# A two-layer graph attention kernel: paired differences on GpSimd in layer 1, and mended orders in four other places

## The reference

```python
# layer 0, 8 heads of 64
data1 = (h @ W.T + b).reshape(N, H, D)
e = src.T[:, :, None] + trg.T[:, None, :]          # per head, N x N
e = where(e >= 0, e, 0.01 * e) + adj[None]          # adj is added, values up to 1e9
x = x + softmax(e) @ data1
# layer 1, 8 heads of 64
adj = maximum(adj, eye(n))
atts = q @ k.T / 8 - 1e16 * (1 - adj)
x = x + sum over heads of softmax(atts) @ values @ Wo
```

## Time and profile before

| | us |
|---|---|
| Median of 3 runs | 4567.05 (4562.28 to 4569.85) |
| The profiled execution, device time | 4565.15 |
| Its span, first to last instruction | 4563.2 |
| Busy PE, DVE, ACT, POOL | 4340.7, 3659.2, 3251.4, 3423.3 |
| Granted TensorE clock, mean | 0.983 |

### The profile page before, as it was taken

How to read it: one execution, slowest core, us unless ns; L and a number is a source line. 1 busy time by engine, 2 the same in 40 slices (tenths; PEclk the granted TensorE clock), 3 DMA queues, 4 the chain that set the end, 5 groups by cost and what they waited for, 6 DMA issues and landing times.

```text
span 4563.2 us, 111741 instructions
## 1 busy us (share of the span) xinstructions
PE 4340.7 (95%) x42956; PEld 2097.1 (46%) x42956; DVE 3659.2 (80%) x7790; ACT 3251.4 (71%) x6022; POOL 3423.3 (75%) x2955
## 2 busy tenths in 40 slices
PE   8699999999999978969999999999999999999998
PEld 4222222222222223425666656656656566566565
DVE  5498998989989854438888888878888878888886
ACT  5366666666666642318888878888878888888886
POOL 2466776677766740009999989989989999899897
PEclk9899999999999989989999999999999999999999
DMA  3566667667666535452333433433433334334333
GB/s 143 138 214 199 201 215 212 215 202 218 222 193 206 158 123 154 118 153 78 114 115 93 127 96 99 135 102 101 120 106 114 111 91 127 107 98 130 100 110 104
DMA packets 464215, 646.06 MB, mean 142 GB/s; under 512 B 49793, under 2 KB 273409, under 8 KB 453569
## 3 DMA queue, kind: packets, MB, share of 16 engines
q1 hardware_dynamic: 385248, 522.36, 37.4%
q10 hardware_dynamic: 73856, 100.83, 7.6%
q0 software_dynamic: 4576, 15.73, 1.2%
HBM read 528.38 MB, written 110.38 MB: 140 GB/s over the span
## 4 chain that ended last, share of the span: by engine, by line
PE 43%; POOL 7%; DVE 2%; ACT 2%; issue 2%; SPq 1%; DMA 0%; DVEq 0%; POOLq 0%; ACTq 0%
PE d_gd L1697 8%; PE d_sc L1713 7%; PE d_sc L1714 7%; POOL d_PL L1484 7%; PE d_sc L1716 4%; PE d_acc L1734 4%; PE d_acc L1736 4%; PE d_acc L1744 4%; PE d_misc L1762 2%; ACT d_PH L1530 1%; DVE d_junk L1570 1%; DVE d_sc L1658 1%; ACT d_PF L1526 0%; PE d_misc L1753 0%; SPq L1373 0%
## 5 line engine op out<-in xcount | busy, mean ns | idle before, releaser
L1484 POOL TENSOR_TENSOR d_PL<-d_PF,d_PH 128x512 f16<-128x512 f32 x2048 | 2314.3, 1165 | 206.1 <-ACT d_PH L1530 202.6
L1570 DVE CUSTOM_DVE_ANT_0 d_junk<-d_gd,d_MR 128x512 bf16<-128x512 f32 x2048 | 1395.7, 687 | 390.8 <-PE d_gd L1697 385.8
L1526 ACT ACTIVATE d_PF<-d_sc 128x512 f32<-128x512 f32 x2048 | 1261.5, 616 | 369.4 <-DVE d_sc L1658 284.3
L1530 ACT ACTIVATE d_PH<-d_sc 128x512 f16<-128x512 f32 x2048 | 1271.3, 621 | 0.0
L818 DVE SCALAR_TENSOR_TENSOR b_P<-R,u,b_A 128x512 f32<-128x512 f32 x1792 | 1195.2, 738 | 68.8 <-PE b_den L871 40.9
L864 PE MATMUL b_acc<-b_P,V 128*64 128x512 f32 x4096 | 956.6, 605 | 66.5 <-DVE b_P L818 58.1
L1713 PE MATMUL d_sc<-d_QA,d_KA 128*128 128x512 f16 x2048 | 776.9, 379 | 41.5 <-ACTq L1501 35.8
L1697 PE MATMUL d_gd<-d_KA,d_QA 128*128 128x512 f16 x2048 | 777.4, 380 | 5.8 <-DVE d_gm L1570 2.6
L1714 PE MATMUL d_sc<-d_QL,d_KB 128*128 128x512 f16 x2048 | 776.4, 379 | 0.0
L1734 PE MATMUL d_acc<-d_V,d_PH 128*128 128x65 f16 x8192 | 638.9, 192 | 1.7 <-ACT d_PH L1530 0.2
L1736 PE MATMUL d_acc<-d_V,d_PH 128*128 128x64 f16 x8192 | 639.8, 193 | 0.0
(11 more groups left out here) (140 smaller groups left out, 4061.6 us busy)
## 6 DMA issues: line engine op xcount, KB each, us to landing
d_V<-scratch_v SPq DMA_DIRECT2D x131, 520.0 KB, 4.3
stage<-in_adjT SPq DMA_DIRECT2D x128, 512.0 KB, 5.1
b_srow<-in_adj ACTq DMA_DIRECT2D x256, 256.0 KB, 4.2
b_rows<-in_adj SPq DMA_DIRECT2D x112, 512.0 KB, 6.6
d_MR<-scratch_mr SPq DMA_DIRECT2D x36, 1024.0 KB, 6.1
d_MT<-scratch_mt SPq DMA_DIRECT2D x35, 1024.0 KB, 6.3
d_KB<-scratch_kh SPq DMA_DIRECT2D x264, 128.0 KB, 3.2
d_KA<-scratch_kh SPq DMA_DIRECT2D x264, 128.0 KB, 3.0
```

Of the source, the lines that this page charges most:

```text
L1484: eng.tensor_tensor(PL[:, t % H_RING, :], PF[:, t % F_RING, :], PH[:, t % H_RING, :], ALU.subtract).then_inc(s_lowp if by_pool(t) else s_l ...
L1526: nc.scalar.activation(PF[:, t % F_RING, :], sc[(nb * TILES + t) % BANKS][:, :], ACT.Exp, scale=EXP_SCALE)
L1530: nc.scalar.activation(PH[:, t % H_RING, :], sc[(nb * TILES + t) % BANKS][:, :], ACT.Exp, scale=EXP_SCALE).then_inc(s_P, 1)
L1570: nc.vector.tensor_tensor_reduce(out=junk[:, gi % 2, :], in0=gd[gi % 2][:, :], in1=MR[:, s, c * QB:(c + 1) * QB], scale=1.0, scalar=-3.0e3 ...
```

## The change

- `layer0_project`: `R` of the first block is loaded behind the fifth chunk's load (`R_LOAD = 4`), and chunks 6 and 7 are both ranked in group 6.
- `layer0_attention`: every `RANK_STEPS` entry is two steps later; the loads stay.
- `layer1_project`: two `hT`; the relus of the next round stand behind the last two query and key tiles, and its transposes and `hT` halves behind the second of the four value products. `MR` is loaded first of all, the first queries and keys ahead of the value stores, and VectorE's `first_mask_rows` stands in the second round.
- `layer1_attention`: GpSimd takes both tiles of a step in one instruction of 1024 columns; `PF` has six tiles. `Wo` is split at steps 30 and 31 of the first head pair and not ahead of the first exponential. The store of a finished block is at step 36 (28 before).

```diff
+    R_LOAD = 4
+    RANKED = [[0], [1], [2], [3], [4], [5], [6, 7], []]
...
-                if g < CHUNKS:
-                    rank_chunk(g)
+                for ci in RANKED[g]:
+                    rank_chunk(ci)
...
-    RANK_STEPS = [3 + 3 * ci // 2 for ci in range(CHUNKS)]
+    RANK_STEPS = [5 + 3 * ci // 2 for ci in range(CHUNKS)]
...
-        hT = sb("c_hT", [P, 2, KC, QB], F16)
+        hT = sb("c_hT", [P, 2, 2, KC, QB], F16)
...
+                    if not last and j >= PAIRS - 2:
+                        for s in range(2):
+                            relu(g + 1, 2 * (j - PAIRS + 2) + s)
...
-                    if not last:
-                        relu(g + 1, s)
+                    if not last and s == 1:
+                        hT_high(g + 1)
...
-    F_RING, H_RING = 4, 8
+    F_RING, H_RING = 6, 8
...
+    HIGH_STEP, LOW_STEP = NT - 2, NT - 1
...
-            pool.sem_inc(s_lowp, PER_RING[1])
+
             for nb in range(NB):
-                for t in range(TILES):
-                    if by_pool(t):
-                        split(nc.gpsimd, pool, nb, t)
+                for step in range(STEPS):
+                    pool.wait_ge(s_P, nb * TILES + (CREDIT + 2 * step + 2))
+                    full = (nb * TILES + 2 * step) % F_RING
+                    half = 2 * step % H_RING
+                    nc.gpsimd.tensor_tensor(PL[:, half:half + 2, :], PF[:, full:full + 2, :], PH[:, half:half + 2, :], ALU.subtract).then_inc(s_lowp, 1)
...
-            act.wait_ge(s_x, 16)
-            act.wait_ge(s_set, 2)
-            nc.scalar.activation(woS[:, 0, :, :], xr[:, :, :], ACT.Copy, scale=W_SCALE).then_inc(s_set, 1)
...
+                        if first and hp * NT + mb == HIGH_STEP:
+                            high_output_weights()
...
-                            act.wait_ge(s_lowp if by_pool(t) else s_low, nb * SPLITS[by_pool(t)] + split_count(t))
-                            nc.scalar.activation(PF[:, t % F_RING, :], sc[(nb * TILES + t) % BANKS][:, :], ACT.Exp, scale=EXP_SCALE)
+                            if nb * TILES + t >= F_RING:
+                                act.wait_ge(s_lowp, nb * STEPS + (t - F_RING) // 2 + 1)
+                            nc.scalar.activation(PF[:, (nb * TILES + t) % F_RING, :], sc[(nb * TILES + t) % BANKS][:, :], ACT.Exp, scale=EXP_SCALE)
...
+                pe.wait_ge(s_lowp, nb * STEPS + step + 1)
                 for x in range(2):
                     t = 2 * step + x
-                    own = by_pool(t)
-                    pe.wait_ge(s_lowp if own else s_low, nb * SPLITS[own] + (PER_RING[own] + split_count(t)))
```

More of the change, by code:

```diff
@@ L140, in _ @@
                 sp.dma_start(rows[:, ci % ROW_RING, :], DR["adj"][s * P:(s + 1) * P, c * CW:(c + 1) * CW]).then_inc(s_row[ci % ROW_RING], 16)
+                if ci == R_LOAD:
+                    sp.wait_ge(s_rout, 16)
+                    for hd in range(H):
+                        sp.dma_start(T["R"][:, 0, hd, :], DR["r"][hd, 0:QB].partition_broadcast(P)).then_inc(T["s_R"], 16)
             for k in range(PREFETCH):
@@ L146, in _ @@
                          allow_slow_non_contiguous=True).then_inc(s_amout, 16)
-            sp.wait_ge(s_rout, 16)
-            for hd in range(H):
-                sp.dma_start(T["R"][:, 0, hd, :], DR["r"][hd, 0:QB].partition_broadcast(P)).then_inc(T["s_R"], 16)
             sp.wait_ge(s_amout, 16)
@@ L955, in load_first_rows, with load_first_queries @@
                     sp.dma_start(MR[:, s, :], DR["mr"][s * P:(s + 1) * P, :]).then_inc(s_MR[s], 16)
[L957 to L965 removed]
+            def load_first_queries(hp):
+                sp.wait_ge(s_qout[hp], 32 * 2)
+                for x in range(2):
+                    row = (2 * hp + x) * D
+                    for half in range(2):
+                        sp.dma_start(QA[half * D:(half + 1) * D, hp, x, :], DR["qh"][row:row + D, 0:QB]).then_inc(s_Q[hp], 16)
+                    sp.dma_start(QL[0:D, hp, x, :], DR["ql"][row:row + D, 0:QB]).then_inc(s_Q[hp], 16)
             def load_first_keys(c):
@@ L1095, in body @@
                                                    in1=hi[:, j % RING, :], op0=ALU.mult, op1=ALU.subtract).then_inc(s_lo, 1)
+                    if g == 1 and j == 0:
+                        first_mask_rows()
                     if g and j - 1 in FIRST_GUARDS:
@@ L1189, in _, with transposes @@
             pe.sem_inc(s_v, 2)
-            def body(g, last):
+            def transposes(g):
                 pe.wait_ge(s_h, g * SUB + SUB)
@@ L1202, in body @@
                     mm.then_inc(s_tp, 1)
+            def body(g, last):
+                if g == 0:
+                    transposes(0)
                 pe.wait_ge(s_hT, g * KC + 2 * KC)
@@ L1225, in body @@
                         for a, b in TERMS:
-                            mm = nc.tensor.matmul(vp[s % 2][:, :], hT[:, a, c, s * P:(s + 1) * P], WS[2][:, b, c, :],
+                            mm = nc.tensor.matmul(vp[s % 2][:, :], hT[:, g % 2, a, c, s * P:(s + 1) * P], WS[2][:, b, c, :],
                                                   start=(c == 0 and a == b == 0), stop=(c == KC - 1 and a == 1))
                     mm.then_inc(s_vp, 1)
+                    if not last and s == 1:
+                        transposes(g + 1)
                 pe.wait_ge(s_lo, g * PAIRS + PAIRS)
@@ L1298, in keys_landed @@
         return 64 * (count + (2 if par == 0 else 1))
-    def by_pool(t):
-        return t % F_RING in POOL_SLOTS
-    def split_count(t):
-        return sum(by_pool(k) == by_pool(t) for k in range(t + 1))
     with ExitStack() as ctx:
@@ L1479, in _ @@
                 sp.wait_ge(s_MR[s], 16 * (NB + 1))
-        def split(eng, engine, nb, t):
-            engine.wait_ge(s_P, nb * TILES + (CREDIT + t + 1))
-            eng.tensor_tensor(PL[:, t % H_RING, :], PF[:, t % F_RING, :], PH[:, t % H_RING, :],
-                              ALU.subtract).then_inc(s_lowp if by_pool(t) else s_low, 1)
         @block.gpsimd
@@ L1647, in body @@
                         for x in range(2):
-                            t = 2 * (step - 1) + x
-                            if t >= 0 and not by_pool(t):
-                                split(nc.vector, dve, nb, t)
-                            elif t < 0 and not first and not by_pool(t + TILES):
-                                split(nc.vector, dve, nb - 1, t + TILES)
                             t = 2 * step + x
@@ L1664, in body @@
                                 guard(nb * HP + (hp + 1), gi, count)
+                        if first and step == LOW_STEP:
+                            low_output_weights()
                         if mb == CROW_STEP:
@@ L1674, in _ @@
                 body(nb, nb == 0)
-            for x in range(2):
-                if not by_pool(TILES - 2 + x):
-                    split(nc.vector, dve, NB - 1, TILES - 2 + x)
             for mb in range(NT):
```

56 lines of the change are left out of this document (24 added, 32 removed).

## The result

The changed kernel takes 4508.21 us in the median of four runs, 4507.14 to 4510.22, against 4568.45 of the kernel before in the same session (4562.28 to 4575.08, four runs). The ratio is 0.9868, with a 95% interval of 0.9851 to 0.9886. That is faster by 60 us; 100 were forecast, and the time lies 11 us above the range. The profiled execution has a span of 4506.0, 57.2 less than the one before.

What follows compares the result with a forecast made beforehand. The prediction took TensorE as the bound, nearly full, with GpSimd close behind. Its terms, -22 - 36 - 41 - 12 + 11 = -100, took the profiled 4565 us to 4465, as a median 4467; the range was 4444 to 4497.

Steps and rivals of the forecast that it cites:

- Layer 0's projection: End of layer 0's projection: `am` lands in time, GpSimd's own end and the barrier then bound; gain 22 us.
- Layer 1's projection: Rounds of layer 1's projection: gaps around the transposes and the second round's waits go; gain 41 us.
- The start: Start of layer 1's attention: TensorE's wait for the `Wo` split goes, until the seventh guard waits for keys; gain 12 us.
- Rival (c): Start of layer 1's attention: won whole, as keys land sooner, 28 us instead of 12, total 4451; chance 0.06.
- The ranks: Layer 0's attention: ranking two steps later removes VectorE's waits for rows and TensorE's stall at step 4; gain 36 us.
- GpSimd's 4 us at the block's end: Layer 0's block ends: later maxima delay `am` and hold GpSimd 4 us; priced at nothing, at most 28 us uncovered.
- The 5 us left for ScalarE's pieces: Layer 0's attention, step 4: 5 us allowed for blocks where ScalarE's mask pieces come late.
- rival (b): Layer 0's wait moves to ScalarE's pieces or `am` at the block's end; gain 15 of 36, total 4488; chance 0.09.
- the prediction's last sign of being wrong: Layer 0's blocks ending with TensorE waiting for `am`'s chain would show the forecast wrong; no size given.
- The difference of 1024 columns: Layer 1's attention: one 2.15 us GpSimd instruction a step, its latency costing 10 us plus 1 in the tail; loss 11.
- the 0.3 us of latency: End of each of 32 head pairs in layer 1's attention: `PL` comes 0.3 us late for TensorE, 10 us in all.
- Rival (a): Layer 1's attention: the pair queues at every head pair's end, 1 us each, 32 in all, total 4488; chance 0.12.

Runs made afterwards that it cites:

- experiment 6: Changed kernel with all four quarters of the second head pair's keys, which the guards read, loaded earlier at the start of layer 1's attention: 4483.29 us, ratio 0.982.
- experiment 7: Changed kernel with layer 0's first six chunks ranked at steps 5 to 10 and the later ones at the steps of the kernel before: 4500.31 us, ratio 0.9858.
- experiment 9: Changed kernel with layer 0's last four ranks one step earlier, in steps 22, 23, 25 and 26: 4497.21 us, ratio 0.9854.
- experiment 1: Changed kernel with only the scaling of the row maxima (`cmh`) in the form with an accumulator: 4467.03 us, ratio 0.9782.
- experiment 2: Changed kernel with GpSimd's difference again in two instructions of 512 columns a step, all else kept: 4462.06 us, ratio 0.9772.
- experiment 4: Changed kernel with both `cmh` and the comparisons for the mask's diagonals in the form with an accumulator: 4455.42 us, ratio 0.9755.
- experiment 5: Changed kernel with `cmh` and the mask-diagonal comparisons in the accumulator form, and the difference in two instructions of 512 columns: 4446.29 us, ratio 0.974.

## Why the prediction was wrong

- **Layer 0's projection**, right in size and reason: `am` in time, the barrier as what is left.
- **Layer 1's projection**, right: -40.3 of -41, from the gaps in the earlier trace rows and their covers.
- **The start**, right in its reason, smaller in size. The prediction let the seventh guard decide and counted as won what this guard wins; but each quarter is waited for on the way (14.8 us in four waits), and the granted clock is 0.90 in this head pair's mean (0.98 before). Rival (c), the start won whole, needed another order of the loads: experiment 6 wins these 18.5 us.
- **The ranks**, mis-sized by one term. The gain of 41 at step 4 was there. What failed is the sentence that prices GpSimd's 4 us at the block's end at nothing because it can make them up: the wait was sized rightly (4.6 us in the mean, 6.5 at most), and 17.3 us of it in seven blocks were not made up, inside the bound of 28 that stood beside it. The 5 us left for ScalarE's pieces didn't come. It is the second half of rival (b), shown by experiments 7 and 9, and the prediction's last sign of being wrong.
- **The difference of 1024 columns**, the step that failed: +11, measured +41.5. Its duration was right (2.145 for 2.15), and GpSimd was not the bound. A wait for `PL` at a head pair's end is there in the size forecast (7.2 us in 28 waits, 0.3 at most), but it is one of weight loads and not of matmuls, and in experiment 1 it goes with the other form of `cmh`, GpSimd's instruction being as long as before. So the 0.3 us of latency that the sum was made of are not shown by themselves; what the pair costs without the lock is 4 us, for the 10 forecast, and 1.4 in the tail, for the 1 forecast. The prediction asked only who waits for GpSimd's result. It didn't ask who waits for GpSimd's *instruction*: `cmh` took 882 ns where 8 numbers take 174, and that row stood in the trace of before. Doubling GpSimd's instruction doubled the wait, at the one place where a mask addition and TensorE's next scores stand behind it. Experiments 1, 2, 4 and 5 give the shares: unpaired, all of it comes back; with both forms changed the pair costs 4 us, 5.4 with the tail, so about 36 of the 41.5 are what the prediction put at nothing, VectorE's small instructions held by GpSimd's long ones. Rival (a) named the place, 1 us a head pair for 1.3 measured, with a queue for a cause; the cause was another. The prediction's 2.05 us, from the Trainium skill, "GPSIMD Engine Reference", section 3.1, doesn't follow from its figure either: a straight line from 1.165 us at 512 columns to 4.497 at 2048 gives 2.28 for 1024 as an estimate, and 2.145 were measured.
- **The chances and the range.** (a) and (b) were two rivals at 0.12 and 0.09. Both places that they named cost time at once: 30 us more than forecast at (a)'s, and 9 of (b)'s 21. The range took them "together" to 4500, but each adds 21 to 4467, which is 4509; the range ended at 4497, below its own rivals' sum, and the measured 4508 lies there. Its middle part is off too: the parts' bounds, added as independent ones (root of the sum of squares), give 4440 to 4498 and not 4448 to 4488.

## What to carry to other kernels

Before an instruction of GpSimd is made longer, look through VectorE's groups for small instructions whose mean is far above their least, and ask what stands behind each of them. Their lateness grew here with the length of GpSimd's instruction, though GpSimd was not the bound; another form of the small instruction can be worth more than the large one's own saving. And a cost that is priced at nothing because an idle engine covers it is to be checked against the whole chain it stands in: the store, the wait for it, the load.

## What the runs showed of the hardware

- A `tensor_scalar` of 128x8 from and to on-chip memory takes 174 ns beside an idle GpSimd, 882 behind instructions of 512 columns and 1718 behind those of 1024. With an accumulator it takes 161 to 163 ns and 83 for reading it, in every kernel that has it. One of 128x128 goes from 604 ns (before) and 1122 (changed), both means, to 342, one of 128x4 took from 157 to 1028 in different kernels, by what ran beside it. A reduction of 128x64 takes 220 throughout.
- Two GpSimd subtractions of 512 columns follow each other at 1.13 us, one of 1024 takes 2.145: 0.06 us a tile is all that pairing saves.
- A store of 2 KB and the load that waits for it were 8.7 us apart in one trace and 9.8 in another. Stages without any change in them differ by up to 6 us from one execution to the next: layer 0's attention with the same ranks took 1418.9 to 1425.2 us in six traces.
